# All five instruction lists of a 16-sequence attention and expert kernel put in another order

## The reference

```python
x = x + attn(layernorm(x))                  # 16 heads of 64, causal softmax
    # inside attn: y = h + heads @ Wo; y = layernorm(y) * gamma + beta
x = x + experts(layernorm(x))
    # logits = h2 @ gate_w.T; top 8 of 32; weights w_e normalised over the 8
    # for each expert: gu = h2 @ guw.T; g, u = split(gu); out += (u * silu(g) @ dw.T) * w_e
```

## Time and profile before

| | us |
|---|---|
| median of three runs (lowest to highest) | 1826.01 (1822.47 to 1826.6) |
| the profiled execution | 1825.31 |
| its span, first to last instruction | 1823.4 |

### The profile page before, as it was taken

The page is one execution under the profiler, slowest core; times in us unless marked ns, Lnnn a source line. Parts: engine busy times, 40 slices in busy tenths (PEclk is TensorE's granted clock), DMA queues, the critical chain, the costliest instruction groups (busy, mean ns, idle before and its releaser), DMA issues.

```text
span 1823.4 us, 54710 instructions
## 1 busy us (share of the span) xinstructions
PE 1720.8 (94%) x20169; PEld 1116.4 (61%) x20169; DVE 1470.7 (81%) x4486; ACT 1428.2 (78%) x2364; POOL 1387.4 (76%) x1161
## 2 busy tenths in 40 slices
PE   4788999999999999999999999999999999999978
PEld 1455566666666666666666666666666666656655
DVE  8877878888887887878788787888888788787547
ACT  3778778787888878788887878888787888877852
POOL 2356787878878788887878789787887978688880
PEclk9899999999999999999999999999999999999999
DMA  6252444526344343633534354343535434253223
GB/s 206 50 123 66 105 114 101 123 62 157 94 108 117 89 123 75 151 101 101 120 86 119 83 144 109 91 120 80 130 88 131 112 94 114 61 135 94 78 65 100
DMA packets 180973, 192.35 MB, mean 105 GB/s; under 512 B 22498, under 2 KB 146274, under 8 KB 180450
## 3 DMA queue, kind: packets, MB, share of 16 engines
q1 hardware_dynamic: 180708, 188.85, 41.5%
HBM read 82.33 MB, written 5.24 MB: 48 GB/s over the span
## 4 chain that ended last, share of the span: by engine, by line
PE 61%; POOL 19%; issue 6%; ACT 6%; DVE 5%; DMA 2%; SPq 1%; ACTq 0%; POOLq 0%; DVEq 0%
PE bank_s L369 12%; PE bank_v L369 12%; PE bank_r L369 12%; POOL p_lo L1451 7%; PE bank_g L369 7%; PE bank_u L369 7%; PE bank_x L369 6%; POOL a_lo L1470 5%; POOL expert_room L1466 5%; PE bank_v L378 3%; ACT p L820 1%; ACT p_hi L758 1%; POOL rstd L1425 1%; DVE max_junk L1087 1%; ACT bank_x L774 1%
## 5 line engine op out<-in xcount | busy, mean ns | idle before, releaser
L1451 POOL TENSOR_TENSOR p_lo<-p,p_hi 128x1280 f16<-128x1280 f32 x256 | 671.8, 2625 | 207.5 <-ACT p_hi L758 207.2
L820 ACT ACTIVATE p<-bank_s,back 128x512 f32<-128x512 f32 (+1 forms) x768 | 456.5, 613 | 75.9 <-PE bank_s L369 37.9
L1087 DVE CUSTOM_DVE_ANT_0 max_junk<-bank_r,mask 128x512 f16<-128x512 f32 (+2 forms) x960 | 427.2, 485 | 73.3 <-PE bank_r L369 68.4
L369 PE MATMUL bank_s<-score_ops 128*128 128x512 f16 (+3 forms) x2048 | 410.9, 302 | 5.1 <-ACT p L820 4.9
L758 ACT ACTIVATE p_hi<-p 128x1280 f16<-128x1280 f32 x256 | 324.2, 1266 | 36.8 <-PE bank_v L369 35.0
L1466 POOL TENSOR_TENSOR expert_room<-expert_room 128x512 f32<-128x512 f32 x240 | 305.4, 1279 | 38.4 <-DVE expert_room L1185 28.5
L1470 POOL TENSOR_TENSOR a_lo<-expert_room,a_hi 128x512 f16<-128x512 f32 x240 | 278.0, 1164 | 15.3 <-ACT a_hi L758 15.1
L369 PE MATMUL bank_v<-v_hi,p_hi 128*128 128x65 f16 x2530 | 256.9, 195 | 5.4 <-DVE oT L1105 3.3
L369 PE MATMUL bank_v<-v_lo,p_hi 128*128 128x64 f16 x2530 | 256.6, 193 | 0.0
L369 PE MATMUL bank_v<-v_hi,p_lo 128*128 128x65 f16 x2530 | 256.3, 194 | 0.0
L369 PEld LDWEIGHTS bank_v<-v_hi,p_hi 128*128 128x128 f16 x2530 | 232.2, 98 | 32.4 <-DVE oT L1105 9.7
(11 more groups left out here) (211 smaller groups left out, 3898.2 us busy)
## 6 DMA issues: line engine op xcount, KB each, us to landing
score_ops<-nat SPq DMA_DIRECT2D x768, 128.0 KB, 2.5
expert_room<-comb_rows SPq DMA_DIRECT2D x480, 128.0 KB, 2.9
xt<-in_x SPq DMA_DIRECT2D x16, 256.0 KB, 3.1
xb<-in_x SPq DMA_DIRECT2D x16, 256.0 KB, 2.9
out_y<-expert_room SPq DMA_DIRECT2D x16, 256.0 KB, 2.7
score_ops<-comb_rows SPq DMA_DIRECT2D x32, 128.0 KB, 3.0
expert_room<-in_gate_up SPq DMA_DIRECT2D x1, 2048.0 KB, 10.6
score_ops<-rowmaxT SPq DMA_DIRECT2D x128, 4.0 KB
```

Of the source, the lines that this page charges most:

```text
L369: return pe.matmul(dst, lhsT, rhs, start=start, stop=stop, skip_group_check=shared)
L820: act.activation(p32[:, h % P_SLOTS, at:at + cols], bank[score_bank(h, u)][:, 0:cols], ACT.Exp, scale=back[:, SC_SCORE:SC_SCORE + 1]).then ...
L1087: done = dve.tensor_tensor_reduce(max_junk[:, k % 2, at:at + cols], bank[b][:, at:at + cols], mask[:, S - cols:S], 1.0, NEG, ALU.add, ALU. ...
L1451: pool.tensor_tensor(p_lo[:, slot, :], p32[:, slot, :], p_hi[:, slot, :], ALU.subtract).then_inc(p_lo_done, 1)
```

## The change

No function, no wait, no buffer and no shape changes. All five lists are replaced by others: the same calls with the same sequence, head and expert numbers (SP 512, PE 2885, ACT 2217, DVE 2585, POOL 880 calls of the lists, in both), in another order, and some with another bank of PSUM (above all in sequences 0 and 15). The turn of the loop also begins at another place of the sequence: for PE at `scores(n, 2, 1)` where it began at `down_product(n - 2, 11)`.

The loop of PE, the part from the end of one sequence's attention to the start of its experts:

```diff
             for n in range(2, B - 2):
-                down_product(n - 2, 11); max_scores(n, 6, 2, R0, R1); scores(n, 1, 1); turn_heads(n - 1, 7, V)
-                up_product(n - 2, 15, U); scores(n, 1, 2); project(n, 14, R0); project(n, 15, R1); down_product(n - 2, 12)
-                down_product(n - 2, 13); times_wo(n - 1, 3, V); max_scores(n, 7, 0, R0, R1); scores(n, 2, 0)
-                down_product(n - 2, 14); scores(n, 2, 1); scores(n, 2, 2); max_scores(n, 7, 1, R0, R1)
-                down_product(n - 2, 15); times_v(n, 0, V); scores(n, 3, 0); max_scores(n, 7, 2, R0, R1); scores(n, 3, 1)
-                times_v(n, 1, V); values(n, 4, R0); scores(n, 3, 2); turn_maxima(n, 3, V); values(n, 5, R1); scores(n, 4, 0)
-                turn_heads(n, 0, V); values(n, 6, R0); scores(n, 4, 1); times_v(n, 2, V); values(n, 7, R1); turn_h2(n - 1)
-                scores(n, 4, 2); times_v(n, 3, V); scores(n, 5, 0); logit_product(n - 1); turn_heads(n, 1, V); scores(n, 5, 1)
-                scores(n, 5, 2); gate_product(n - 1, 0, G); scores(n, 6, 0); times_wo(n, 0, V); scores(n, 6, 1)
-                scores(n, 6, 2); turn_h(n + 1, V); up_product(n - 1, 0, U); scores(n, 7, 0); turn_weights(n - 1)
-                project(n + 1, 0, R0); project(n + 1, 1, R1); times_v(n, 4, V); scores(n, 7, 1)
-                max_scores(n + 1, 0, 0, R0, R1); scores(n, 7, 2); gate_product(n - 1, 1, G); up_product(n - 1, 1, U)
-                max_scores(n + 1, 0, 1, R0, R1); times_v(n, 5, V); gate_product(n - 1, 2, G); scores(n, 8, 0)
-                max_scores(n + 1, 0, 2, R0, R1); scores(n, 8, 1); up_product(n - 1, 2, U); project(n + 1, 2, R0)
...
+                scores(n, 2, 1); down_product(n - 2, 13); scores(n, 2, 2); max_scores(n, 7, 1, R0, R1); times_v(n, 0, V)
+                scores(n, 3, 0); down_product(n - 2, 14); down_product(n - 2, 15); scores(n, 3, 1)
+                max_scores(n, 7, 2, R0, R1); scores(n, 3, 2); times_v(n, 1, V); values(n, 4, R0); scores(n, 4, 0)
+                values(n, 5, R1); scores(n, 4, 1); turn_maxima(n, 3, V); turn_heads(n, 0, V); scores(n, 4, 2); scores(n, 5, 0)
+                values(n, 6, R0); scores(n, 5, 1); times_v(n, 2, V); turn_h2(n - 1); times_v(n, 3, V); logit_product(n - 1)
+                scores(n, 5, 2); turn_heads(n, 1, V); scores(n, 6, 0); values(n, 7, R1); scores(n, 6, 1); times_wo(n, 0, V)
+                gate_product(n - 1, 0, G); scores(n, 6, 2); turn_h(n + 1, V); scores(n, 7, 0); up_product(n - 1, 0, U)
+                turn_weights(n - 1); project(n + 1, 0, R0); project(n + 1, 1, R1); times_v(n, 4, V); scores(n, 7, 1)
+                scores(n, 7, 2); max_scores(n + 1, 0, 0, R0, R1); gate_product(n - 1, 1, G); up_product(n - 1, 1, U)
+                scores(n, 8, 0); max_scores(n + 1, 0, 1, R0, R1); scores(n, 8, 1); times_v(n, 5, V); gate_product(n - 1, 2, G)
+                max_scores(n + 1, 0, 2, R0, R1); scores(n, 8, 2); up_product(n - 1, 2, U); project(n + 1, 2, R0)
...
```

The same part of ACT's list:

```diff
             for n in range(2, B - 2):
-                exps(n, 2, 0); exps(n, 2, 1); exps(n, 2, 2); p_high(n, 2); exps(n, 3, 0); residual_apply(n - 1); exps(n, 3, 1)
-                exps(n, 3, 2); v_high(n, 4, R0); copy_maxima(n, 3, V); p_high(n, 3); v_high(n, 5, R1); o_high(n, 0, V)
-                exps(n, 4, 0); v_high(n, 6, R0); second_apply(n - 1); exps(n, 4, 1); h2_high(n - 1); exps(n, 4, 2)
-                p_high(n, 4); exps(n, 5, 0); o_high(n, 1, V); exps(n, 5, 1); exps(n, 5, 2); v_high(n, 7, R1); route(n - 1)
-                exps(n, 6, 0); p_high(n, 5); exps(n, 6, 1); h_high(n + 1, V); gate_tanh(n - 1, 0, G); exps(n, 6, 2)
-                copy_weights(n - 1); qk_high(n + 1, 0, R0); qk_high(n + 1, 1, R1); exps(n, 7, 0); p_high(n, 6); exps(n, 7, 1)
...
+                unit_high(n - 2, 15); exps(n, 2, 1); exps(n, 2, 2); exps(n, 3, 0); p_high(n, 2); exps(n, 3, 1)
+                residual_apply(n - 1); exps(n, 3, 2); p_high(n, 3); exps(n, 4, 0); exps(n, 4, 1); copy_maxima(n, 3, V)
+                v_high(n, 4, R0); v_high(n, 5, R1); o_high(n, 0, V); exps(n, 4, 2); second_apply(n - 1); v_high(n, 6, R0)
+                h2_high(n - 1); exps(n, 5, 0); exps(n, 5, 1); p_high(n, 4); o_high(n, 1, V); exps(n, 5, 2); route(n - 1)
+                v_high(n, 7, R1); p_high(n, 5); exps(n, 6, 0); exps(n, 6, 1); h_high(n + 1, V); gate_tanh(n - 1, 0, G)
+                exps(n, 6, 2); copy_weights(n - 1); qk_high(n + 1, 0, R0); qk_high(n + 1, 1, R1); exps(n, 7, 0); p_high(n, 6)
...
```

The same part of DVE's list:

```diff
-                row_maximum(n, 7, 0, 0, R0); row_maximum(n, 7, 0, 1, R1); residual_stats(n - 1); row_maximum(n, 7, 1, 0, R0)
-                row_maximum(n, 7, 1, 1, R1); denominators(n, 0, V); divide(n, 0, V); add_experts(n - 2)
+                row_maximum(n, 6, 2, 1, R1); gate_times_tanh(n - 2, 15, G); times_up(n - 2, 15, U); o_low(n - 1, 7, V)
+                qk_low(n, 14, R0); qk_low(n, 15, R1); input_stats(n + 2); row_maximum(n, 7, 0, 0, R0)
+                row_maximum(n, 7, 0, 1, R1); add_heads(n - 1, 3, V); residual_stats(n - 1); denominators(n, 0, V)
+                row_maximum(n, 7, 1, 0, R0); divide(n, 0, V); row_maximum(n, 7, 1, 1, R1); add_experts(n - 2)
                 row_maximum(n, 7, 2, 0, R0); row_maximum(n, 7, 2, 1, R1); denominators(n, 1, V); divide(n, 1, V)
-                add_input(n - 1); second_stats(n - 1); v_low(n, 4, R0); v_low(n, 5, R1); o_low(n, 0, V); input_stats(n + 2)
-                denominators(n, 2, V); v_low(n, 6, R0); divide(n, 2, V); h2_low(n - 1); denominators(n, 3, V); divide(n, 3, V)
-                take_logits(n - 1); choose(n - 1); o_low(n, 1, V); mark_chosen(n - 1); add_heads(n, 0, V); weigh(n - 1)
-                h_low(n + 1, V); v_low(n, 7, R1); gate_times_tanh(n - 1, 0, G); qk_low(n + 1, 0, R0); qk_low(n + 1, 1, R1)
...
```

and of POOL's:

```diff
             for n in range(2, B - 2):
-                weigh_unit(n - 2, 10); unit_low(n - 2, 9); weigh_unit(n - 2, 11); split_maxima(n, 2); weigh_unit(n - 2, 12)
-                unit_low(n - 2, 10); p_low(n - 1, 14); unit_low(n - 2, 11); p_low(n - 1, 15); unit_low(n - 2, 12)
-                weigh_unit(n - 2, 13); p_low(n, 0); unit_low(n - 2, 13); weigh_unit(n - 2, 14); weigh_unit(n - 2, 15)
-                unit_low(n - 2, 14); unit_low(n - 2, 15); p_low(n, 1); residual_inverse(n - 1); split_maxima(n, 3)
-                p_low(n, 2); second_inverse(n - 1); p_low(n, 3); p_low(n, 4); p_low(n, 5); p_low(n, 6); weigh_unit(n - 1, 0)
...
-                unit_low(n - 1, 4); p_low(n, 9); p_low(n, 10); unit_low(n - 1, 5); split_maxima(n + 1, 1)
-                weigh_unit(n - 1, 7); p_low(n, 11); weigh_unit(n - 1, 8); unit_low(n - 1, 6); p_low(n, 12); add_beta(n)
-                unit_low(n - 1, 7); weigh_unit(n - 1, 9); p_low(n, 13); unit_low(n - 1, 8)
-
...
```

```diff
-                place_qk(n, 6); spread_weights(n - 2, 14); spread_weights(n - 2, 15); place_qk(n, 7); place_max(n, 2)
-                load_x(n + 2); store(n - 2); keep_weights(n - 1); spread_weights(n - 1, 0); spread_weights(n - 1, 1)
-                spread_weights(n - 1, 2); place_qk(n + 1, 0); spread_weights(n - 1, 3); place_qk(n + 1, 1); place_max(n, 3)
-                spread_weights(n - 1, 4); spread_weights(n - 1, 5); spread_weights(n - 1, 6); place_qk(n + 1, 2)
-                spread_weights(n - 1, 7); place_qk(n + 1, 3); spread_weights(n - 1, 8); place_max(n + 1, 0); load_xb(n)
...
```

The end of the lists of PE and POOL:

```diff
-            times_v(15, 15, R0); turn_heads(15, 6, V); turn_heads(15, 7, R0); down_product(14, 12); down_product(14, 13)
-            times_wo(15, 3, V); down_product(14, 14); down_product(14, 15); turn_h2(15); logit_product(15)
-            up_product(15, 0, S1); gate_product(15, 0, R1); gate_product(15, 1, G); up_product(15, 1, U); turn_weights(15)
-            gate_product(15, 2, S0); gate_product(15, 3, R1); gate_product(15, 4, G); up_product(15, 2, S1)
...
+            up_product(14, 15, U); times_v(15, 15, V); turn_heads(15, 6, R0); turn_heads(15, 7, V); down_product(14, 12)
+            times_wo(15, 3, R0); down_product(14, 13); down_product(14, 14); down_product(14, 15); turn_h2(15)
+            logit_product(15); gate_product(15, 0, S0); gate_product(15, 1, R1); gate_product(15, 2, G); up_product(15, 0, S1)
+            up_product(15, 1, U); gate_product(15, 3, S0); gate_product(15, 4, R1); turn_weights(15); up_product(15, 2, S1)
+            gate_product(15, 5, G); up_product(15, 3, U); gate_product(15, 6, S0); up_product(15, 4, S1); up_product(15, 5, U)
...
-            p_low(15, 13); weigh_unit(14, 12); unit_low(14, 11); p_low(15, 14); weigh_unit(14, 13); p_low(15, 15)
-            unit_low(14, 12); unit_low(14, 13); weigh_unit(14, 14); weigh_unit(14, 15); unit_low(14, 14); unit_low(14, 15)
-            residual_inverse(15); second_inverse(15)
...
+            p_low(15, 12); weigh_unit(14, 9); weigh_unit(14, 10); unit_low(14, 8); p_low(15, 13); unit_low(14, 9)
+            weigh_unit(14, 11); p_low(15, 14); unit_low(14, 10); unit_low(14, 11); p_low(15, 15); weigh_unit(14, 12)
```

(2 more changed lines are left out.)

1028 lines of the change are left out of this document (521 added, 507 removed).

## The result

| | before | after |
|---|---|---|
| median of the runs side by side, us | 1825.01 (1822.47 to 1826.6) | 1797.21 (1795.87 to 1802.81) |
| ratio, 95% interval | | 0.9855 (0.983 to 0.988) |
| profiled execution, us | 1825.31 | 1795.87 |
| its span, us | 1823.4 | 1794.1 |

What follows compares the result with a forecast made beforehand. PE was taken to bound the loop, with the norm chain meeting its bank waits; 4.8 (loop) + 2 (start) + 1 (end) = 7.8 us off the profiled execution, 1818.2 at the median, predicted 1818, range 1801 to 1831.

Steps and rivals of the forecast that it cites:

- The loop: Twelve turns, 268.5 to 1557 us: walked waits of 1.9 us a turn against 2.3, so 4.8 us off.
- The 0.5 us at `logit_product`: Loop, turn_h2 to logit_product: a new wait of 0.5 us in each turn, bounds 0.4 to 0.7.
- More cover under the norm chain: Loop, PE's work between times_wo(n - 1, 3) and turn_h2(n - 1): 13.6 us for 12.3, 1.3 more.
- Up to 97 us: Start: DVE's work is the longest and the new list has all of it too; 0, bounds -3 and +3.
- 97 to 200 us: Sequence 1's norm chain passage, with a list nearly that of the loop: 2 us off, bounds -5 and +2.
- The end: Sequences 14 and 15: POOL's 0.96 us idle until residual_stats(15) goes, 1 us off; PE's 10.3 us standstill stays.
- The last stretch: Gates first, DVE no longer between routing and tanh; PE idles 6.4 us; taken as 0, bounds -2 and +2.
- C: Rival: nothing waits in a turn, 21.6 us off in the loop and 3 to 5 outside: 1800; chance 0.16.
- E: Rival: PE's busy time is no floor, mixed order shortens each turn by 1.6 us more: 1799; chance 0.03.
- B: Rival: no change, the norm chain decides and the loop keeps 107.2 us a turn: 1822.4 to 1829.6; chance 0.20.
- D: Rival: slower, banks V and XB take back more than R0 gives, waits of 2.6 us a turn: 1833; chance 0.18.
- The sign named in advance: Start: new waits elsewhere, or more than 3 us more or less before 268 us, would show the forecast wrong.

Runs made afterwards that it cites:

- e2: New order on all five engines for the calls from 285 to 1557 us (the loop), old order before and behind: 1822.78 us for 1824.47.
- e8: Changed kernel with scores(n, 4, 2) and scores(n, 5, 0) put between turn_maxima(n, 3) and turn_heads(n, 0) on PE: 1798.57 us, ratio 0.9853.
- e4: New order on all five engines for the calls up to 97 us, old order behind: 1819.32 us for 1824.47.
- e15: Kernel before with rest(6) on DVE moved behind row_maximum(0, 7, 2, 1), denominators(0, 1) and divide(0, 1): 1822.43 us for 1824.4.
- e17: New order for the calls from 74 to 97 us alone, the rest in the old order: 1823.93 us for 1824.53.
- e13: Kernel before with p_high(15, 5) moved on ACT alone to directly behind exps(15, 5, 2): 1825.42 us for 1824.4.
- e6: Changed kernel with project(1, 2) put back directly behind project(1, 1), with its consumers and the old banks of two max_scores: 1800.99 us, ratio 0.9867.
- e16: Changed kernel with project(2, 0) put back on PE directly behind scores(1, 6, 2): 1797.45 us, ratio 0.9853.
- e7: New order for the calls from 1557 to 1690 us (sequence 14) alone, old order before and behind: 1819.86 us for 1824.72.
- e18: New order for the calls from 160 to 285 us alone, the rest in the old order: 1820.91 us for 1824.53.
- e12: Old order up to 1690 us, new order for the calls from there on: 1820.83 us for 1825.81.
- e3: Old order up to 1557 us, new order from there on (sequences 14 and 15): 1816.33 us for 1824.47.
- e11: Changed kernel with 2.4 us more work on DVE, two unread reductions ahead of rest(3): 1801.4 us, ratio 0.9873.
- e5: Kernel before with project(1, 2) moved behind scores(0, 8, 0) on PE and its two consumers as much later: 1827.13 us for 1824.72.
- e9: Kernel before with POOL's p_low(0, 1), (0, 2) and (0, 4) made to wait for DVE's rest(4), (6) and (10): 1826.5 us for 1825.81.
- e10: Kernel before with 2.4 us more work on DVE, two unread reductions ahead of rest(3): 1827.47 us for 1825.81.
- e1: New order on all five engines for the calls up to 285 us, old order from there on: 1809.64 us for 1824.47.

## Why the prediction was wrong, and where it was right

**The loop, 4.8 us: near in number, 3.5, and partly by luck.** 3.5 us by the two traces, 2.7 in e2. The wait at `turn_heads(n, 0)` became 1.4 us (forecast 1.1, bounds 0.65 to 1.9) and the one at `values(n, 6)` is gone, both as forecast. The 0.5 us at `logit_product` did not come. But the sum of waits was the wrong thing to count. The walk made 2.3 us of the old turn and 1.9 of the new; PE's idle time in a turn is 1.9 in both, so the new order was walked rightly and the old one 0.4 too high, and this 0.4 was the whole term. e8, which fills the largest wait, changes nothing. More cover under the norm chain was forecast, 1.3 us, and came as 0.75, but the chain, forecast as equal, is 0.5 us longer. What is left of it, 0.2 us less idle time in that passage, is lost again behind it, and the 0.2 that the turn gained is PE's busy time, which the forecast held constant. Why that fell is open. The forecast turn of 106.8 came from a single old turn of 107.20; the mean of ten is 107.36, and the new one 107.15.

**Up to 97 us, 0 (bounds -3 and +3): failed, 5 to 6 us.** The step was "the new list has all of it too", DVE's load taken for the time of the stretch. That the order up to there gives the time is shown by e4, 5.2 us (2.9 to 6.4) with that piece alone. DVE's 45.8 of 54 us left 8.2 us idle, 3.1 in the new order, and 4.3 of the 45.8 were themselves spent blocked by POOL; this idle time was the room to be costed. e15 gives 2.0 of the 5 to one move, `rest(6)` behind the last row maxima. e17, the new order from 74 to 97 us alone, gives 0.6 and so not the whole. Which moves ahead of 74 us give the rest, or whether they need each other, is open.

A second reading of this stretch stands beside it, and no run separates them. The forecast left the clock out of the term, though it named it (0.84). It was halved for 17.1 of the 54 us before and for 3.4 of the 47.6 after, which is worth at most 6.8 us of PE's time, and PE's busy time fell by 6.6 while its idle time stayed. The clock may follow from the better order or add to it. A bound comes from the traces with a full clock from 75 us to turn_h(1): 94.9 us (e13, old list) against 90.6 to 91.4 (changed kernel, e6, e8, e16), so some 4 of the 6 us are there without that part of the clock, an estimate from one trace of the old list.

**97 to 200 us, 2 (bounds 5 less and 2 more): failed, 7.4.** The idle time of 12.1 us was read and most of it left standing, because the loop has 1.8 in such a passage. Shown are 2.1 for `project(1, 2)` in the new surroundings (e6) and 0.9 for `project(2, 0)` (e16), both by their traces alone. Part of it is the clock, below.

**200 to 289 us and 1557 to 1700 us: not costed at all.** The sum went from 97 to 200 and from 1700 on. The two stretches left out gave 3.6 and, up to turn_h2(14), 4.6 us (e7: 4.9; e18, which includes the passage ahead of it: 3.6). This is the plainest fault: about 8 of the 20 us missed stood in no term, though 1557 to 1700 has some 10 us of PE's idle time.

**The end, 1: failed, 2.0 between turn_h2(14) and turn_h2(15).** The 0.96 us of the earlier trace rows went as forecast, and the 10.3 us in which PE stands still became 9.1. But "from 1700 to 1767 POOL works 66.0 of 67 us" was a window cut at the edge of a hole (and it holds the low parts of eleven heads, not ten). The run begins at 1694, and what decides is when it begins (e7) and, as e12 suggests, that it has no hole; e13 could not take the hole away alone. The 2.0 us are not in every execution: with the same new list e12 and four others need 89.5 to 89.8 us from turn_h2(14) to turn_h2(15), but e3, e8 and e11, whose clock was halved for 6.8 us around turn_h2(14), need 91.5 to 91.8, as much as before (91.5).

**The last stretch, 0 (bounds -2 and +2): 2.1 less,** at the edge of its bounds; 1.7 in e12.

**The rivals.** C (1800) and E (1799) named times near the measured one, for reasons that are not there. In C nothing waits in a turn; it still waits 1.6 us. For E, a shorter turn by a better mixed PE, a turn has 0.2 us less busy time where E wanted 1.6: the sign is there, about a tenth of the size, and e8 shows the busy time growing by as much as the idle time shrank. So the premise that PE's work of 1720.8 us stays holds to 0.3% in the loop and no better. B's time did not come, nor D's. With E the rule of the Trainium skill (Perfetto Trace Analysis, Identifying the Most-Contended Engine) has little support here: weight loads are busy 65% of the new turn, and the turn is hardly nearer to that limit. The sign named in advance as against the forecast, more than 3 us less before 268 us, is the one that came, with 13.5 by 205 us.

## What to carry to other kernels

Cost every stretch in which the bounding engine idles, and take its idle time as the room of a new order; the forecast came near where the engine was full and was off by a factor where it wasn't. Measure a walked chain in the old trace before trusting the difference of two walks. Let a window begin where the run of work begins, not at a round number, and read an engine's durations against their like before calling its busy time work. In a kernel that is one long mesh of lists, putting one piece back costs what its stall shows, but moving one piece forward mostly renames the wait: of four such moves (e5, e8, e13, e15) one gained.

## What the runs showed of the hardware

DVE and POOL shut each other out in some operations (2.08, 2.95 and 3.08 us for 1.27, each beside a `p_low`). Besides these three of `rest`, an operation of 7x7 elements, whose like takes 0.22 us, took 1.88 in the changed kernel, and ended with the `p_low` beside it (DVE, then POOL):

```profile
52.78 1.88 DVE L1015 TENSOR_SCALAR w_diagonal<-ident,w_peak 7x7 f32<-7x7 f32 x1
```

```profile
52.02 2.61 POOL L1449 TENSOR_TENSOR p_lo<-p,p_hi 128x1280 f16<-128x1280 f32 x1 [1.19 <-DVE w_lo L1030]
```

It goes the other way too: one `p_low` after took 3.63 us beside `rest`, for 2.62. Up to 113 us before, no operation of DVE that reads a bank was over 0.06 us longer than its like. The Trainium skill (SBUF — State Buffer, Who interferes with whom) says that DVE and GpSimd share one pair of ports to SBUF under an exclusive lock, so that the later one blocks until the first is done, and that a DVE instruction with two inputs from SBUF contends with a GpSimd instruction that reads SBUF. `rest` has two such inputs, and these rows agree. By which rule the operation of 7x7 elements, with one tensor and a scalar, is caught they don't tell. What the lock is worth no row tells: in e9 the engine made to wait instead, POOL, was on the path just as much.

The clock falls at places that the list doesn't fix. The rows are 74 to 113 us in the kernel before and in e13, which has the same order there; the third number from the right is the granted clock:

```profile
74.00:113.00 39.00, 30.57 (x337) 19.01 (x333) 27.50 (x76) 25.92 (x40) 16.71 (x9) 0.87 0.34 70
```

```profile
74.00:113.00 39.00, 29.92 (x372) 18.50 (x369) 29.52 (x85) 27.49 (x42) 17.56 (x9) 0.96 0.39 81
```

At 0.87 (10.2 of the 39 us at 1.2 GHz, the rest at 2.4) scores(0, 8, 2) ends at 111.3, at 0.96 (3.4 us) at 109.7; in the new order the clock is full in that stretch and it ends at 100.1. So 6.8 us less at half clock went with 1.6 us, and all 10.2 would at this rate be 2.4 of the 11 gained by there, an estimate from these two traces. Nor is the full clock a fixed thing of the new order: in e1 and e4, with the new list up to 97 us, it was halved for 3.4 us at 80 us and turn_h(1) ended 1.9 us later than in the changed kernel. It came with PE's longest idle time (10.3 and 9.1 us in the norm chain of sequence 15, with 0.67 and 0.74 granted) but not with each piece of it: the stall of 2.2 us in e6 left the clock at 2.4 GHz.
